# Attention scores in a fused cross-attention kernel: from stacked high and low parts to four unsplit float32 matmuls in the row strips of the array

## The reference

```
xq  = ada_ln(x_q, t_vec, Wss_q, bss_q)          # (1 + scale) * normalised + bias
xkv = ada_ln(x_kv, t_vec, Wss_kv, bss_kv)
q = (xq @ Wq + bq).reshape(B, Lq, 16, 32)
kv = (xkv @ Wkv + bkv).reshape(B, Lkv, 2, 16, 32);  k, v = kv[:, :, 0], kv[:, :, 1]
scores = einsum('bqhd,bkhd->bhqk', q, k) / sqrt(32)
attn = softmax(scores, axis=-1)
out = einsum('bhqk,bkhd->bqhd', attn, v).reshape(B, Lq, 512)
return x_q + (out @ Wp + bp)
```

## Time and profile before

| | |
|---|---|
| median of 3 runs | 2374.38 us (2374.38 to 2377.04) |
| profiled execution: span | 2371.8 us, and some 2.6 us around it |
| TensorE matmul busy | 2308.8 us, 97% of the span |
| VectorE busy | 1936.1 us, 82% |
| ScalarE busy | 1806.9 us, 76% |
| DMA | 211.65 MB, mean 89 GB/s |
| mean granted TensorE clock | 0.986 of full speed |

### The profile page before, as it was taken

One profiled execution on the slowest core, in us unless ns is written; L12 is line 12 of the kernel. 1 busy time (PEld: TensorE's weight loads), 2 busy tenths in 40 slices (PEclk: granted clock), 3 DMA queues, 4 the chain that ended last, 5 costly groups with the idle time before them and its releaser, 6 DMA issues.

```text
span 2371.8 us, 34855 instructions
## 1 busy us (share of the span) xinstructions
PE 2308.8 (97%) x12234; PEld 1028.5 (43%) x12234; DVE 1936.1 (82%) x1153; ACT 1806.9 (76%) x1822; POOL 62.2 (3%) x46
## 2 busy tenths in 40 slices
PE   7998799999999999999998999999999999999998
PEld 3456344444443444444443444444443334444343
DVE  4564588888889888888887888898888988888886
ACT  1333588888888888888887888888888977777772
POOL 1111000000001000000001000000001000000000
PEclk9999799999999999999999999999999999999999
DMA  6777911111117211111137111111154222332223
GB/s 231 265 267 259 185 54 54 54 53 53 52 27 147 65 54 54 54 44 54 53 72 158 54 54 35 35 47 53 53 114 92 68 60 67 95 94 78 72 60 127
DMA packets 135663, 211.65 MB, mean 89 GB/s; under 512 B 15016, under 2 KB 48296, under 8 KB 135532
## 3 DMA queue, kind: packets, MB, share of 16 engines
q1 hardware_dynamic: 124572, 186.70, 29.1%
q0 software_dynamic: 3376, 12.85, 1.7%
q10 hardware_dynamic: 7584, 10.49, 1.2%
HBM read 138.18 MB, written 71.82 MB: 89 GB/s over the span
## 4 chain that ended last, share of the span: by engine, by line
PE 85%; issue 1%; POOL 1%; ACT 1%; DVE 1%; DMA 0%; SPq 0%; ACTq 0%; POOLq 0%; DVEq 0%
PE ring L890 33%; PE o_ps L905 32%; PE l_ps L964 4%; PE l_ps L973 4%; PE l_ps L985 4%; PE l_ps L926 1%; POOL g_max L859 1%; PE ring L985 1%; PE o_ps L911 1%; PE l_ps L923 1%; PE ring L878 1%; ACT pt L1126 1%; DMA vg<-v_full 0%; DVE acc L1202 0%; DVE s_max L1213 0%
## 5 line engine op out<-in xcount | busy, mean ns | idle before, releaser
L1126 ACT ACTIVATE pt<-ring,shift 128x1024 f32<-128x1024 f32 x1600 | 1678.5, 1120 | 312.5 <-PE ring L890 296.4
L1202 DVE TENSOR_TENSOR acc<-acc,pt 128x2048 f32<-128x2048 f32 x672 | 1516.7, 2288 | 104.4 <-ACT pt L1126 104.0
L890 PE MATMUL ring<-qs,ks 128*128 128x512 f32 x3200 | 1005.2, 436 | 18.9 <-ACT pt L1126 18.9
L905 PE MATMUL o_ps<-pt,vg 128*32 128x512 f32 x6400 | 855.6, 607 | 0.0
L890 PEld LDWEIGHTS ring<-qs,ks 128*128 128x128 f32 x3200 | 563.2, 189 | 470.8 <-ACT pt L1126 306.2
L1202 DVE TENSOR_TENSOR acc<-pt 128x2048 f32<-128x2048 f32 x64 | 146.7, 2292 | 140.6 <-ACT pt L1126 140.6
L905 PEld LDWEIGHTS o_ps<-pt,vg 128*32 128x32 f32 x6400 | 126.2, 108 | 294.7 <-issue 225.7
L973 PEld LDWEIGHTS l_ps<-work 128*128 128x128 f32 x672 | 86.0, 190 | 121.6 <-issue 121.6
L964 PE MATMUL l_ps<-work 128*128 128x256 f32 x336 | 117.4, 431 | 0.0
L973 PE MATMUL l_ps<-work 128*128 128x128 f32 x672 | 114.0, 297 | 0.0
L331 PE MATMUL bank<-xt,wq 128*128 128x512 f32 x256 | 111.9, 595 | 0.0
(11 more groups left out here) (79 smaller groups left out, 670.1 us busy)
## 6 DMA issues: line engine op xcount, KB each, us to landing
qs<-q_split SPq DMA_DIRECT2D x128, 256.0 KB, 5.0
ks<-k_split SPq DMA_DIRECT2D x80, 320.0 KB, 6.6
work<-ctx_t SPq DMA_DIRECT2D x21, 1024.0 KB, 7.6
k_split<-work SPq DMA_DIRECT2D x42, 256.0 KB, 2.1
x_bias<-xb ACTq DMA_DIRECT2D x8, 1024.0 KB, 9.1
q_split<-hi SPq DMA_DIRECT2D x8, 1024.0 KB, 9.2
q_split<-lo SPq DMA_DIRECT2D x8, 1024.0 KB, 11.2
o_sums<-o_sb SPq DMA_DIRECT2D x32, 256.0 KB, 7.4
```

What stands on the lines that cost most here:

```text
L890: mm = nc.tensor.matmul(ring[:, bank + i, :], ks[:, h, t * P:(t + 1) * P], qs[U.par][:, h, :], start=True, stop=not exact)
L905: mm = nc.tensor.matmul(o_ps[cols, :], vg[:, t, cols], pt[t % PR][:, h, :], start=(t == 0), stop=False, skip_group_check=True)
L1126: nc.scalar.activation(pt[t % PR][:, 2 * pair:2 * pair + 2, :], ring[:, bank:bank + 2, :], ACT.Exp, scale=SCALE, bias=bias[:, :]).then_inc ...
L1202: nc.vector.tensor_tensor(a[:, :, :], (pt[t - 1] if k <= 2 else a)[:, :, :], pt[t % PR][:, :, :], ALU.add).then_inc(p_added, 1)
```

## The change

The scores are computed from unsplit float32 q and k. `ks` holds the 32 channels of head h on the partitions 32h to 32h+31, `qs` likewise, and the four heads of a tile are four matmuls of 32 rows each, in the four row strips of the array, each into its own PSUM bank. Four float32 matmuls are eight instructions. With the split go:

- the high and low tiles and their copies: the prologue's hi on ACT and lo on DVE become one DVE add of the bias; in the attention stage ACT's `split_hi` becomes `take_k` and DVE's `split_lo` goes
- half of the stored q and k, and three quarters of the loaded: one DMA instead of four for q and for each chunk of k
- four tail matmuls become one, with the tail keys of the four heads block by block in 8 columns

The order changes with it. `scores(U, t)` issues a whole tile, both items, behind one wait for the items up to 2t - 2. A step of `unit` is now `scores(t + 1)`, `weigh(t)`, `side(t)`; the last step has the tail, `weigh(24)`, the next unit's `scores(nxt, 0)`, and then the weighing of the tail. The sample at the end of a group is made one head a step, at t = 18, 19, 20 and 21, and DVE reduces it after its add of t = 22. The exact pass is changed alike (not shown).

```diff
-                        bias = bk_c if b.kv else bq_c
-
-                        act.wait_ge(split_out[b.par], START + 32 * b.use)
-                        for m in range(b.m_tiles):
-                            act.wait_ge(proj_done, START + b.results + m + 1)
-                            src = bank[:, 4 + (2 * b.par if b.kv else m), :]
-                            nc.scalar.activation(hi[b.par][:, m, :], src, ACT.Identity,
-                                                 bias=bias[:, m:m + 1]).then_inc(hi_ready, 1)
...
+                        dve.wait_ge(qk_out[b.par], START + 16 * b.use)
                         for m in range(b.m_tiles):
-
-                            dve.wait_ge(hi_ready, b.splits + m + 1)
+                            dve.wait_ge(proj_done, START + b.results + m + 1)
                             src = bank[:, 4 + (2 * b.par if b.kv else m), :]
-                            nc.vector.scalar_tensor_tensor(out=lo[b.par][:, m, :], in0=src, scalar=bias[:, m:m + 1],
-                                                           in1=hi[b.par][:, m, :].bitcast(F32),
-                                                           op0=ALU.add, op1=ALU.subtract).then_inc(lo_ready, 1)
+                            nc.vector.tensor_scalar(qk[b.par][:, m, :], src, bias[:, m:m + 1], None,
+                                                    ALU.add).then_inc(qk_ready, 1)
...
-            ks = sb("ks", [P, HG, NT * P], F32R)
-            kt = sb("kt", [P, HG * SEL], F32R)
+            ks = sb("ks", [P, NT * P])
+            kt = sb("kt", [P, HG * TAIL])
...
-            qs = [sb(f"qs{i}", [P, HG, QB], F32R) for i in range(2)]
+            qs = [sb(f"qs{i}", [P, QB]) for i in range(2)]
...
-            def tail_of(t, h):
-                return t[:, h * P:(h + 1) * P]
+            def rows_of(h):
+                return slice(h * DH, (h + 1) * DH)
 
             def load_q(sp, g, U):
 
                 sp.wait_ge(o_ready, START + U.u - 1)
-                for r in range(4):
-                    src = q_dram[r % 2, ds(g * P, P), ds(U.b * QB, QB)].rearrange("(h d) q -> d h q", d=DH)
-                    sp.dma_start(qs[U.par][r * DH:(r + 1) * DH, :, :].bitcast(F32), src).then_inc(q_in[U.par], 16)
+                sp.dma_start(qs[U.par][:, :], q_dram[ds(g * P, P), ds(U.b * QB, QB)]).then_inc(q_in[U.par], 16)
 
             def load_keys(sp, g, G, parts=range(NC)):
                 for c in parts:
 
                     sp.wait_ge(pv_done, START + (G * NB - 1) * NT + CT * (c + 1))
                     keys = slice(c * CT * P, (c + 1) * CT * P)
-                    for r in range(4):
-                        src = k_dram[r // 2, ds(g * P, P), keys].rearrange("(h d) k -> d h k", d=DH)
-                        sp.dma_start(ks[r * DH:(r + 1) * DH, :, keys].bitcast(F32), src).then_inc(k_in[c], 16)
+                    sp.dma_start(ks[:, keys], k_dram[ds(g * P, P), keys]).then_inc(k_in[c], 16)
                     sp.dma_start(vg[:, c * CT:(c + 1) * CT, :],
...
-                for r in range(4):
-                    src = k_dram[r // 2, ds(g * P, P), NT * P:LKV].rearrange("(h d) k -> d h k", d=DH)
-                    dst = kt[r * DH:(r + 1) * DH, :].rearrange("p (h c) -> p h c", c=SEL)[:, :, 0:TAIL]
-                    sp.dma_start(dst.bitcast(F32), src).then_inc(tail_in, 16)
                 for h in range(HG):
+                    sp.dma_start(kt[rows_of(h), h * TAIL:(h + 1) * TAIL],
+                                 k_dram[ds(g * P + h * DH, DH), NT * P:LKV]).then_inc(tail_in, 16)
...
-                sp.wait_ge(lo_done, START + T.t + 1)
-                sp.dma_start(k_dram[0, rows, cols], k_hi).then_inc(k_out, 16)
-                sp.dma_start(k_dram[1, rows, cols], k_lo).then_inc(k_out, 16)
+                sp.wait_ge(k_done, START + T.t + 1)
+                sp.dma_start(k_dram[rows, cols], k_st).then_inc(k_out, 16)
...
-                def scores(U, n, first):
-
-                    bank = 2 * (n % RING)
-                    if n >= RING:
-
-                        pe.wait_ge(e_done, scores_done(U, n - RING))
-                    elif not first:
-                        pe.wait_ge(e_done, U.u * ITEMS + n - RING + 1)
-                        if n == 0 and U.starts_group:
-                            pe.wait_ge(k_in[0], 80 * (U.G + 1))
-                    if n == 0:
-                        pe.wait_ge(q_in[U.par], 64 * (U.use + 1))
-                    if n == ITEMS - 1:
-                        if U.starts_group and not exact:
-                            pe.wait_ge(tail_in, 128 * (U.G + 1))
+                def scores(U, t, first=False):
+
+                    if not first:
+
+                        pe.wait_ge(e_done, U.u * ITEMS + 2 * t - 1)
+                    if t == 0:
+                        pe.wait_ge(q_in[U.par], 16 * (U.use + 1))
+                    if U.starts_group and not exact and t % CT == 0:
+                        pe.wait_ge(k_in[t // CT], 32 * (U.G + 1))
+                    for h in range(HG):
+                        n, i = divmod(2 * t * 2 + h, 2)
+                        rows = rows_of(h)
+                        mm = nc.tensor.matmul(ring[:, 2 * (n % RING) + i, :], ks[rows, t * P:(t + 1) * P],
+                                              qs[U.par][rows, :], start=True, stop=not exact)
+                        if i == 1 and not exact:
+                            mm.then_inc(s_ready, 1)
+                    if exact:
                         for h in range(HG):
-                            mm = nc.tensor.matmul(ring[:, bank, :], tail_of(kt, h), qs[U.par][:, h, :],
-                                                  start=(h == 0), stop=(h == HG - 1 and not exact))
-                        if exact:
-                            for h in range(HG):
-                                mm = nc.tensor.matmul(ring[:, bank, :], tail_of(row_tail, h), m_row[0:1, h, :],
-                                                      start=False, stop=(h == HG - 1))
-                    else:
-                        t, pair = divmod(n, 2)
-                        if U.starts_group and not exact and pair == 0 and t % CT == 0 and t > 0:
-                            pe.wait_ge(k_in[t // CT], 80 * (U.G + 1))
-                        for i in range(2):
-                            h = 2 * pair + i
-                            mm = nc.tensor.matmul(ring[:, bank + i, :], ks[:, h, t * P:(t + 1) * P],
-                                                  qs[U.par][:, h, :], start=True, stop=not exact)
-                            if exact:
-                                mm = nc.tensor.matmul(ring[:, bank + i, :], row1[0:1, :], m_row[0:1, h, :],
-                                                      start=False, stop=True)
+                            n, i = divmod(2 * t * 2 + h, 2)
+                            rows = rows_of(h)
+                            mm = nc.tensor.matmul(ring[:, 2 * (n % RING) + i, :], row1[rows, :], m_row[rows, :],
+                                                  start=False, stop=True)
+                            if i == 1:
+                                mm.then_inc(s_ready, 1)
+
+                def tail_scores(U):
+
+                    bank = 2 * ((ITEMS - 1) % RING)
+                    pe.wait_ge(e_done, U.u * ITEMS + ITEMS - RING)
+                    if U.starts_group and not exact:
+                        pe.wait_ge(tail_in, 128 * (U.G + 1))
+                    mm = nc.tensor.matmul(ring[0:HG * TAIL, bank, :], kt[:, :], qs[U.par][:, :],
+                                          start=True, stop=not exact)
+                    if exact:
+                        mm = nc.tensor.matmul(ring[0:HG * TAIL, bank, :], row_tail[:, :], m_row[:, :],
+                                              start=False, stop=True)
                     mm.then_inc(s_ready, 1)
...
                 def unit(U, nxt, side):
 
                     for t in range(NT):
-                        for n in (2 * t + RING, 2 * t + RING + 1):
-                            if n < ITEMS:
-                                scores(U, n, exact)
-                            elif nxt is not None:
-                                scores(nxt, n - ITEMS, False)
+                        if t < NT - 1:
+                            scores(U, t + 1)
+                        else:
+                            tail_scores(U)
                         weigh(U, t)
                         if t == NT - 1:
+                            if nxt is not None:
+                                scores(nxt, 0)
                             weigh_tail(U)
                         side(t)
-                    if nxt is not None:
-                        scores(nxt, RING - 1, False)
-
-                def sample(G):
-
-                    pe.wait_ge(q_in[0], 64 * (Unit(G, 0, 0).use + 1))
-                    pe.wait_ge(k_in[0], 80 * (G + 1))
-
-                    pe.wait_ge(l_taken, START + Unit(G, 0, 0).u - 1)
+
+                def first_sample():
+
```

(61 more changed lines are left out.)

93 lines of the change are left out of this document (46 added, 47 removed).

## The result

The changed kernel takes 2492.28 us (2491.58 to 2493.21), the kernel before 2374.38 us on the same chip. The ratio is 1.0493, 95% interval 1.0479 to 1.0508. The profiled execution has a span of 2489.9 us against 2371.8: +118.1 us, where the prediction summed up +125.

The account below looks back on a forecast made before the run. PE's order of work was taken to bound the kernel. Task units 76, output units 19, other units 23, the sample 15 and the start -8 made +125 us on 2374.4: 2499 us, range 2420 to 2600, leaving 0.2 out.

Parts of the forecast that it names:

- The score block: Scores of a tile on PE: four row strips run side by side, loads included, in 1.07 us (bounds 1.05 to 1.40).
- loads in a row: Rival, score block: the four weight loads don't overlap, +0.33 us in PE-bound steps; 2691 us, 2595 if half overlaps; chance 0.14.
- no overlap: Rival, score block: the row strips follow one another, 3.6 us a tile; 4500 us in all; chance 0.03.
- the other price, 1.12 us: Score block by a skill rule, row tiles 3.07 times as fast as unpacked: 1.12 instead of 1.07 us, +24 us.
- The modes: Full-array side work between column and row strips: one more load and mode change, 0.19 us a step, less 0.06 gained.
- a free change: Rival, mode borders: row strips and full array need no drain between them, 78 us less, 2421 us; chance 0.09.
- faster: Rival, strip borders: neither drain nor exposed load, DVE's adds bound the unit, about 2190 us; chance 0.06.
- The ring: Plain steps: scores wait for an exponential, a chain of 2.33 us against 2.13, +0.20 us a step.
- The task unit: A unit with a task grows by 3.6 us, 64.07 to 67.7; 21 units, +76 us.
- The start: Start of the attention stage: 0.9 MB of loads take 4.4 us instead of 12.8, -8 us.
- The clock: Rival, plain steps: 0.26 us of idle lowers the granted clock, 4.1 us a step, 3080 us; chance 0.03.
- the sample: Group boundaries: sample moved past three steps, POOL taking 10.86 us, ACT waits 9.0 us instead of 3.9; +15 us.

Follow-up runs that it names:

- experiment 4: Changed kernel with the projection of k issued as four matmuls of 32 weight columns, in the column strips of the weighing: 2470.22 us, ratio 1.0393.
- experiment 5: Projections of k and v and most output products in column strips, on the kernel before (`stacked_columns`), 2403.91 us, and on `strips_ahead`, 2401.26 us.
- experiments 1 and 2: `strips_ahead` and `split_wait`, in that order: 2461.0 us and 2464.48 us.
- experiment 6: Kernel before, with the sample and its all-reduce two steps later: 2375.61 us; or with VectorE waiting for the all-reduce before further adds: 2359.14 us.
- experiment 3: Kernel before, stacked scores kept, with a tile's scores issued together behind one wait, one tile ahead: 2393.44 us, ratio 1.0073.
- strips_ahead: Changed kernel with the score order and waits of the kernel before, pairs up to three items ahead, each behind its own wait: 2461.0 us, ratio 1.0354.
- stacked_columns: Kernel before with only its side work changed: projections of k and v and most output products in four column strips: 2403.91 us, ratio 1.0124.
- split_wait: Changed kernel with the one wait ahead of a tile's scores split, pair 0 waiting for one exponential earlier: 2464.48 us, ratio 1.0375.

## Why the prediction held, and which step failed

- **The score block** of four row strips was the unknown that I feared most. It is 1.07 us, as taken. The rivals of loads in a row and of no overlap fall, and so does the other price, 1.12 us.
- **The modes.** 0.19 us for each border, less 0.06: the steps came out at 2.69 and 2.93 us to the hundredth, and experiment 4 shows the term by itself. The rival of a free change falls. So does "faster": it needs borders at nothing. With the side work's borders gone (experiment 5) strips still don't pay in the order tried.
- **The ring.** 2.34 us for 2.33. By the rows the longer plain steps make some 75 us; experiments 1 and 2, which loosen the chain and don't remove it, gain 31 and 28.
- **The task unit** is 67.47 us for 67.7.
- **The start** gave -8.7 us for -8.
- **The clock** fell in the changed kernel's attention stage, behind its start, only for four stretches of 3.4 us behind stalls: two at the loop's end, one behind the second boundary, one behind the first unit with output products. It never fell for the 0.21 us that TensorE is idle in each plain step.
- **Failed: the sample.** I added "3 x 5.1 = +15 us" with "POOL 10.86". I took the duration of a row as the instruction's work and moved it along the time axis. It was a wait for VectorE's adds, 10.86 us long behind five of them; the changed kernel reduces the sample three steps later, two adds are left, and it takes 2.05 to 2.14 us. The trace that I read had the warning. At the start of the attention stage, with no adds beside it, the same instruction takes 0.38 us (256.42, experiment 6). The boundaries cost +1.4 us in place of +29, since the changed kernel also shed the stall that the kernel before has.
- **Left out: the loop's end,** about 13 us of the task units, which no term held. Two causes seem to add up: TensorE has no scores ahead of it at the jump (experiment 3, 5.3 us there), and its program no longer stays on the chip (experiment 5; 5.9 us in `strips_ahead`). The second is argued from packets and program length, not shown by a run that shortens the program.
- **Mis-sized: units without the loop.** In the last group plain steps are 2.42 us, not 2.34, with 0.31 us of ScalarE's idle time ahead of its exponential where the loop has 0.22. It makes some 0.08 x 20 = 1.6 us in a unit without side work (+6.7 for the predicted 4.6). Why ScalarE starts later there no run tells. A unit with output products is +4.65 for 3.2; its steps with products are +0.13 to +0.16, near the forecast, its plain steps and its end are longer.

That the total came within 7 us owes something to errors that cancel: 28 us too much at the boundaries and 4 behind the attention stage, 11 too little in the task units and 14 in the last group.

## What to carry to other kernels

Count the changes of array mode in a step, not only the columns streamed: strips saved 0.06 us a tile and paid 0.19 us wherever full-array work stands between strips of the two kinds. A pair of strips takes as long as four, so an order that leaves an odd pair pays for it. When the work ahead of an engine is cut, look at the places where it was needed (an order's plain steps, a unit's end, a loop's jump) and ask whether the longer program still stays on the chip. And before the duration of a GpSimd row is used in a sum, see whether its end is tied to another engine's: one wait in the right place made the kernel before 0.7% faster, where the whole change made it 4.9% slower.

## What the runs showed of the hardware that I had not expected

- Four float32 matmuls of 32 rows and 512 columns in four row strips take 1.07 us with their loads, and two of them 1.06 us (`strips_ahead`); four of 32 columns of weights and 256 columns take less than the full-array pair they replace beside strips (0.61 us of busy time for 0.70, and a border less: 0.19 us in the step).
- With 15386 instructions or more, packets of instructions kept coming in the loop (15 to 20 of 16 KB in 240 us; none with 12234). Read as a reload of TensorE's program, it made the jump back cost up to 3.2 us of standing still, and in `stacked_columns` 3.4 or 6.8 us at half clock followed.
- An all-reduce of one column takes 0.35 us. Behind a run of VectorE's adds it was kept waiting 6.5 and 10.9 us, through three and five of them. What decides whether it gets in between two adds is open: in `split_wait` it got in though the next add's input had been ready 0.48 us before that add (781.68 to 782.16).
